# A vision tower on one core: an expert's bias fold summed on VectorE over eight row blocks, then one TensorE product

## The chip, the cores and the metric

The kernel runs on one core of a Trainium2 chip. The metric is device time in microseconds, the median of several executions. The profile comes from one further execution. Its engines are named PE (TensorE), PEld (TensorE's weight loads), DVE (VectorE), ACT (ScalarE), POOL (GpSimd) and SP (SyncE).

## The reference

The input is 64 images; each gives 196 tokens of 256 numbers, 12,544 tokens in all. What is computed, cut to what matters:

```
h  = patches(x) @ W_tok.T + b_tok                      # 768 -> 256
h1 = h + ssm(layernorm(h))                             # Bu, a scan over tokens, y = xs@C + u@D
x2 = layernorm(h1)
y1 = ln1(x2 + mha(x2))                                 # attention over the 64 images, 4 heads
t  = y1[tokens of expert e]                            # top 1 of 8 experts, capacity 1568
hid = t @ w1[e] + b1[e]                                # 256 -> 1024, no activation follows
y  = hid @ w2[e] + b2[e]                               # 1024 -> 256
out = h1 + ln2(y1 + gate * y)
```

Since nothing stands between the two products of an expert, the kernel folds them beforehand: `W12[e] = w1[e] @ w2[e]` (256 x 256), and `b12[e] = b1[e] @ w2[e] + b2[e]` (256). The change is about the second.

## The kernel before

The program has three stages, with a barrier between them: tokens, scan and layer norms (the first, up to about 560 us of the profile), attention and routing, then the experts. Each stage is one block in which every engine runs its own stream of instructions, and semaphores join them. The order on an engine is the order in which its `step` function lists the parts.

The first stage goes over 49 groups of 256 tokens (`NG`), one group per round. An engine's `step(k)` treats several groups at different ages: TensorE in round k turns u of group k-2 into ps_t (L650), makes the outputs ps_y of group k-4, the tokens ps_h of group k in two halves, then a part of a fold (`fold`), then the inputs of the scan ps_b of group k-2. The products of the groups are sums of three fp32r products each (high and low parts), by `product` (L297). In the same round VectorE makes, in this order: nrm_x (L595, L599), the scans xs (L531), the residual h1o from ps_y (L578), nrm_a (L564, L568), ul (L523), h of the first half (L549) and its statistics, sl (L539), the statistics of h1o and mv_xa (L591), h of the second half, its statistics and aggregates (L559). ScalarE makes nrm_x (L438) behind mv_xa, bu from ps_b (L414), xh (L402), sh, uh, x2o and u. GpSimd makes xl in three instructions of 128x512 (L476), hb (L484) and h1b (L492). TensorE needs ul before ps_b, sl before ps_y of the next round, and u before the next ps_t.

The fold runs beside this, six rounds per expert (`FOLD = 6`), for 48 rounds. `k.slot(FOLD)` is the place in the six, called slot here, and `k.turn(FOLD)` the expert. The weights of an expert lie in w1s (w1 transposed) and w2s, 128 partitions x 8 blocks of 256, with b1 behind it as eight columns. Slots 0 and 1 make the first half of W12 in ps_f (four products each, L690), slots 2 and 3 the second. Slots 4 and 5 make the bias: eight products (four each, L694) with the weights b1p (128x2, one column of b1 doubled) and one block of w2s as moving operand, summed into ps_fb (2x256). These products are plain fp32, and each shows in the profile as two records. b1p is copied from w2s by GpSimd in slot 2 (`pair_b1`, L501). The result is added into b12 by VectorE at the end of slot 0 of the next expert (`fold_bias`, L607).

SyncE loads the next expert (`next_expert`): w1s in slot 4 after the last ps_f product; the first half of w2s in slot 5, after slot 4's bias products (`fb_first`); the second half in slot 0, after slot 5's (`fb_ps`). Each of these stands in SyncE's order ahead of the round's xf load and of the two stores of h1b and x2o.

Of the kernel before, what the change touches and what calls it, by code (L numbers as in the profile page):

```python
# [13 lines left out]
P = 128  # L14
# [86 lines left out]
def build(nc, xt, w_tok, b_tok, log_a, w_b, b_b, w_c, b_c, w_d, b_d, log_dt, w_in, b_qk, b_v, w_o, b_o,  # L101
# [4 lines left out]
    with ExitStack() as ctx:  # L106
# [22 lines left out]
        c_eps = sb("c_eps", [P, 1])  # L129
        before = sb("before", [P, P], BF16)  # L130
# [24 lines left out]
        with ExitStack() as pre:  # L155
# [73 lines left out]
            def _(dve):  # L229
# [9 lines left out]
                v.memset(c_eps[:], EPS)  # L239
                v.memset(ones_b[:], 1.0)  # L240
# [63 lines left out]
        with ExitStack() as pa:  # L304
# [26 lines left out]
            b1p = sb("b1p", [P, FK, 2], F32, pa)  # L331
# [14 lines left out]
            b1_pair, w2_first, fb_first = (sem(n) for n in ("fold_b1_pair", "w2_first_loaded", "fold_bias_half"))  # L346
# [5 lines left out]
            def _(sp):  # L352
# [18 lines left out]
                def next_expert(k):  # L371

                    if k.slot(FOLD) == 4:
                        wait(sp, fold_ps, k.turn(FOLD) + 1)
                        sp.dma_start(w1s[:], w1t[k.turn(FOLD) + 1]).then_inc(w1_loaded, 16)
                    elif k.slot(FOLD) == 5:
                        wait(sp, fb_first, k.turn(FOLD) + 1)
                        sp.dma_start(w2s[:, 0:HALF], w2[k.turn(FOLD) + 1, :, 0:HALF]).then_inc(w2_first, 16)
                    elif k.slot(FOLD) == 0:
                        wait(sp, fb_ps, k.turn(FOLD))  # L380
                        sp.dma_start(w2s[:, HALF:], w2[k.turn(FOLD), :, HALF:]).then_inc(w2_loaded, 16)
# [84 lines left out]
            def _(pool):  # L466
# [28 lines left out]
                def pair_b1(k):  # L495
                    if k.slot(FOLD) == 2 and k.valid(FOLD * NE):
                        e = k.turn(FOLD)
                        wait(pool, w2_loaded, (e + 1) * 16)
                        wait(pool, fb_ps, e)
                        apart(pool, passed["pool"])  # L500
                        nc.gpsimd.tensor_copy(b1p[:], w2s[:, FK * D:FK * D + FK].unsqueeze(2)  # L501
                                              .to_broadcast([P, FK, 2])).then_inc(b1_pair, 1)

                def step(k):
                    pair_b1(k)
# [10 lines left out]
            def _(dve):  # L516
# [84 lines left out]

                def fold_bias(k):
                    if k.slot(FOLD) == 0 and k.back(1).valid(FOLD * NE):
# [14 lines left out]
                def step(k):  # L618

                    for m, stage in ((k.back(5), scale_x), (k.back(5), shift_x), (k.back(3), of(scan, 0)),  # L620
# [3 lines left out]
                                     (k, of(hidden, 1)), (k, of(stats_h, 1)), (k, of(mean_h, 0)), (k, of(mean_h, 1)),  # L624
                                     (k, fold_bias)):
                        if m.valid(NG):
                            stage(m)

# [3 lines left out]
            def _(pe):  # L632
# [42 lines left out]
                def fold(k):  # L675
# [22 lines left out]
                    if k.slot(FOLD) == 4:  # L698
                        last.then_inc(fb_first, 1)
                    if k.slot(FOLD) == 5:  # L700
                        last.then_inc(fb_ps, 1)

                def step(k):
# [4 lines left out]
                    if k.valid(NG):  # L708
                        tokens(k, 0)
                        tokens(k, 1)  # L710
                    if k.valid(FOLD * NE):
                        fold(k)
# [817 lines left out]
```

## Time and profile before

| | us |
|---|---|
| median of 3 runs | 1353.25 (1352.43 to 1354.72) |
| the profiled execution | 1356.27 |
| its span, first to last instruction | 1354.4 |
| TensorE busy | 1261.2 (93%) |
| VectorE busy | 1020.7 (75%) |
| ScalarE busy | 737.2 (54%) |
| GpSimd busy | 718.3 (53%) |

Busy times of one engine add up only where its instructions do not overlap; those of different engines run side by side. TensorE's instructions are pipelined: one lasts longer than the distance from its start to the next start, so rounds and folds are measured from start to start. The rounds of the steady part are read in the timeline, each from its ps_t on.

### The profile page before, as it was taken

The numbers are of one execution on the slowest core, as the hardware profiler recorded it, in microseconds if no ns is written. First come the engines' busy times: TensorE is split into PE (matmuls) and PEld (weight loads), VectorE is DVE, ScalarE is ACT, GpSimd is POOL, SyncE is SP. The second block draws the span as 40 slices with busy tenths as digits, with TensorE's granted clock in tenths as the row PEclk, the third lists the DMA queues.
The fourth block names the chain that finished last, engine by engine and source line by source line (L and its number), as shares of the span: only waits on it lengthen the run. The fifth ranks groups of instructions, "written<-read, shape, count | busy, mean of one in ns | idle before, by whom it ended". The sixth has DMA issues, their size and how long they took to land. (4 is left out here: it accounts for less than half of the span.)

```text
span 1354.4 us, 37450 instructions
## 1 busy us (share of the span) xinstructions
PE 1261.2 (93%) x11810; PEld 1147.7 (85%) x11811; DVE 1020.7 (75%) x2787; ACT 737.2 (54%) x1515; POOL 718.3 (53%) x966
## 2 busy tenths in 40 slices
PE   2999999999999999589999999999999984999995
PEld 1999999999999999489999999999999983666663
DVE  4577778887777787747777777777777765699997
ACT  3455555555555555445555555555555541477775
POOL 1655666666656665303444444444444443277776
PEclk9999999999999999889999999999999985999998
DMA  7435454545454543202223322332223224677773
GB/s 235 147 121 168 149 163 132 163 137 178 145 182 117 178 117 98 96 28 83 96 93 101 101 93 96 99 99 95 93 97 101 97 79 133 183 215 234 226 230 121
DMA packets 97044, 180.07 MB, mean 133 GB/s; under 512 B 12319, under 2 KB 62497, under 8 KB 95970
## 3 DMA queue, kind: packets, MB, share of 16 engines
q1 hardware_dynamic: 82244, 138.66, 34.1%
q0 software_dynamic: 13312, 39.75, 8.0%
q10 hardware_dynamic: 1440, 1.07, 0.3%
q8 instruction: 23, 0.38, 0.1%
q14 instruction: 25, 0.20, 0.1%
HBM read 112.69 MB, written 67.80 MB: 133 GB/s over the span
## 5 line engine op out<-in xcount | busy, mean ns | idle before, releaser
L476 POOL TENSOR_TENSOR xl<-xf,xh 128x512 fp32r<-128x512 f32 x141 | 179.2, 1299 | 204.6 <-ACT xh L402 204.6
L297 PE MATMUL ps_h<-wh,xh 128*128 128x256 f32 x588 | 166.3, 283 | 4.9 <-DVE xl L611 4.9
L297 PE MATMUL ps_h<-wh,xl 128*128 128x256 f32 x588 | 166.2, 283 | 0.0
L297 PE MATMUL ps_h<-wl,xh 128*128 128x256 f32 x588 | 166.0, 282 | 0.0
L851 ACT ACTIVATE zn<-z,nm_z,rs_z 128x256 f32<-128x256 f32 x98 | 53.6, 594 | 200.7 <-DVE nm_z L982 200.7
L1323 POOL DMA_INDIRECT out<-res,c_idx x106 | 116.5, 1099 | 61.6 <-issue 46.2
L920 POOL DMA_INDIRECT bins<-rows,slot_i x98 | 100.7, 1028 | 60.1 <-POOL slot_i L914 45.2
L1471 PE MATMUL c_ps_y<-w,yt 128*128 x424 | 116.9, 398 | 6.5 <-issue 4.1
L297 PEld LDWEIGHTS ps_h<-wh,xh 128*128 128x128 f32 x588 | 111.8, 190 | 5.7 <-DVE xl L611 5.7
L297 PE MATMUL b<-x2h,wh 128*128 128x256 f32 x392 | 114.7, 293 | 0.0
L297 PEld LDWEIGHTS ps_h<-wl,xh 128*128 128x128 f32 x588 | 111.7, 190 | 0.0
L297 PEld LDWEIGHTS ps_h<-wh,xl 128*128 128x128 f32 x588 | 111.5, 190 | 0.0
L297 PE MATMUL b<-x2h,wl 128*128 128x256 f32 x392 | 110.8, 283 | 0.0
L297 PE MATMUL b<-x2l,wh 128*128 128x256 f32 x392 | 110.7, 282 | 0.0
L936 DVE TENSOR_TENSOR x2l<-ps_o,x2h 128x512 fp32r<-128x512 f32 x49 | 33.9, 692 | 96.5 <-ACT x2h L856 96.5
L894 POOL TENSOR_TENSOR x2b<-x,rows_c 128x512 f32<-128x512 f32 x49 | 63.4, 1295 | 62.3 <-DVE z L968 58.5
L914 POOL CAST slot_i<-small 128x2 int32<-128x2 f32 x49 | 9.1, 186 | 159.3 <-DVE small L1030 159.3
L1471 PEld LDWEIGHTS c_ps_y<-w,yt 128*128 128x128 f32 x424 | 71.9, 189 | 24.4 <-issue 12.0
L438 ACT ACTIVATE nrm_x<-mv_xa,c_eps 128x2 f32<-128x2 f32 x49 | 14.5, 296 | 141.3 <-DVE mv_xa L591 141.3
L531 DVE TENSOR_TENSOR_SCAN xs<-decay,xs,bu 128x256 f32<-128x256 f32 x96 | 66.9, 738 | 29.8 <-ACT bu L414 29.5
L492 POOL TENSOR_TENSOR h1b<-h1o,rows_c 128x512 f32<-128x512 f32 x49 | 79.4, 1622 | 10.1 <-DVE h1o L578 10.1
L539 DVE TENSOR_TENSOR sl<-xs,sh 128x512 fp32r<-128x512 f32 x49 | 79.8, 1629 | 0.1
(255 smaller groups left out, 4409.4 us busy)
## 6 DMA issues: line engine op xcount, KB each, us to landing
xf<-xt SPq DMA_DIRECT2D x49, 768.0 KB, 5.3
row<-bins SPq DMA_DIRECT2D x106, 257.5 KB
h_dram<-h1b SPq DMA_DIRECT2D x49, 256.0 KB, 5.3
x_dram<-x2o SPq DMA_DIRECT2D x49, 256.0 KB, 5.4
x<-x_dram SPq DMA_DIRECT2D x98, 128.0 KB, 2.8
rows<-h_dram SPq DMA_DIRECT2D x98, 128.0 KB, 2.8
w1s<-w1t SPq DMA_DIRECT2D x8, 1024.0 KB, 6.8
w2s<-w SPq DMA_DIRECT2D x8, 516.0 KB, 5.4
```

The lines of the kernel that those rows point to most:

```text
L297: last = nc.tensor.matmul(out_ps, a, b, start=(i == 0), stop=(i == len(terms) - 1))
L438: nc.scalar.activation(nrm_x[:, 0, :], mv_x[:, :, 1], ACT.Sqrt, bias=c_eps[:]).then_inc(x_sd, 1)
L476: last = nc.gpsimd.tensor_tensor(xl[:, p, part], xf[:, p, part], xh[:, p, part].bitcast(F32), ALU.subtract)
L492: nc.gpsimd.tensor_tensor(h1b[:, p], h1o[:, p], r_be2.unsqueeze(1).to_broadcast([P, 2, D]), ALU.add).then_inc(h1b_done, 1)
L531: v.tensor_tensor_scan(xs[:, p, t, :], decay[:, t, bass.ds(m.n() * G % N, G)], bu[:, p, t, :], 0.0 if first else xs[:, 1 - p, t, G - 1:G], ...
L539: v.tensor_tensor(sl[:, p, :], xs[:, p].rearrange("p t g -> p (t g)"), sh[:, p, :].bitcast(F32), ALU.subtract).then_inc(s_lo, 1)
L851: A(zn[:, s, :], z[:, s, :], ACT.Identity, bias=nm_z[:, s:s + 1], scale=rs_z[:, s:s + 1]).then_inc(Q["zn"], 1)
L894: g.tensor_tensor(x2b[:, p], x2[:, p], r_bo.unsqueeze(1).to_broadcast([P, 2, D]), ALU.add).then_inc(Q["x2b"], 1)
L920: g.indirect_dma_start(bins, bass.IndirectOffsetOnAxis(ap=slot_i[:, p, s:s + 1], axis=0), rows[:, p, s, :], None).then_inc(scattered[p], 16)
L936: v.tensor_tensor(xl[:], b_2, xh[:].bitcast(F32), ALU.subtract).then_inc(Q["x2lo"], 1)
L1323: g.indirect_dma_start(out, bass.IndirectOffsetOnAxis(ap=idx[:, b, i:i + 1], axis=0), res[:, b, i, :], None, bounds_check=S - 1, oob_is_er ...
L1471: mm(ps_y[p][:, i, :], yt[:, p, i, t * P:(t + 1) * P], w12[:, bass.ds(e, 1), t * D:(t + 1) * D].rearrange("p a d -> p (a d)"), start=(t == ...
```

## The change

The sum over the eight row blocks moves off TensorE. VectorE keeps an array acc (128x256). In slots 2 to 5 it does two of eight steps each, `acc = w2s[block f] * b1[f] + acc`, with b1's column as a scalar per partition; the first is a plain product. This part, `sum_bias`, stands first in VectorE's round. TensorE then needs a single product, weights `ones_2` (128x2, all ones) and acc as moving operand, which sums over the partitions (`fold_sum`). It stands in slot 0 of the next expert, ahead of `fold`. `fold_bias` goes from the end of slot 0 to the end of slot 1. GpSimd's `pair_b1` goes. SyncE's two w2s loads wait for the counts of `acc_done` in place of the bias products. The diff, cut to its core:

```diff
+                def sum_bias(k):
+                    if k.slot(FOLD) >= 2 and k.valid(FOLD * NE):
+                        e = k.turn(FOLD)
+                        if k.slot(FOLD) == 2:
+                            wait(dve, w2_first, (e + 1) * 16)
+                            wait(dve, w2_loaded, (e + 1) * 16)
+                            wait(dve, fb_ps, e)
+                        for f in range((k.slot(FOLD) - 2) * 2, (k.slot(FOLD) - 1) * 2):
+                            w, b = w2s[:, f * D:(f + 1) * D], w2s[:, FK * D + f:FK * D + f + 1]
+                            if f == 0:
+                                v.tensor_scalar(acc[:], w, b, None, ALU.mult).then_inc(acc_done, 1)
+                            else:
+                                wait(dve, acc_done, e * FK + f)
+                                v.scalar_tensor_tensor(acc[:], w, b, acc[:], ALU.mult, ALU.add).then_inc(acc_done, 1)
...
                 def fold_bias(k):
-                    if k.slot(FOLD) == 0 and k.back(1).valid(FOLD * NE):
+                    if k.slot(FOLD) == 1 and k.back(2).valid(FOLD * NE):
                         e = k.turn(FOLD) - 1
                         wait(dve, fb_ps, e + 1)
...
-                    if k.slot(FOLD) == 4:
-                        wait(pe, fb_out, e)
-                        wait(pe, b1_pair, e + 1)
-                    for f in range(again * FK // 2, (again + 1) * FK // 2):
-                        if part < FT:
+                    if part < FT:
+                        for f in range(again * FK // 2, (again + 1) * FK // 2):
                             last = nc.tensor.matmul(ps_f[:, part * D:(part + 1) * D],
                                                     w1s[:, f * D + part * P:f * D + (part + 1) * P],
                                                     w2s[:, f * D:(f + 1) * D], start=(f == 0), stop=(f == FK - 1))
-                        else:
-                            last = nc.tensor.matmul(ps_fb[:], b1p[:, f, :], w2s[:, f * D:(f + 1) * D],
-                                                    start=(f == 0), stop=(f == FK - 1))
...
+                def fold_sum(k):
+                    if k.slot(FOLD) == 0 and k.back(1).valid(FOLD * NE):
+                        e = k.turn(FOLD) - 1
+                        wait(pe, acc_done, (e + 1) * FK)
+                        wait(pe, fb_out, e)
+                        nc.tensor.matmul(ps_fb[:], ones_2[:], acc[:], start=True, stop=True).then_inc(fb_ps, 1)
...
                     elif k.slot(FOLD) == 5:
-                        wait(sp, fb_first, k.turn(FOLD) + 1)
+                        wait(sp, acc_done, k.turn(FOLD) * FK + FK // 2)
...
                     elif k.slot(FOLD) == 0:
-                        wait(sp, fb_ps, k.turn(FOLD))
+                        wait(sp, acc_done, k.turn(FOLD) * FK)
```

The lines shift: L297 is L299 in the changed kernel, L690 is L695, L549 is L541, L595 is L587.

TensorE, slot 4, between the last tokens and the inputs of the scan; before:

```order
L297 MATMUL ps_h<-wl,xh 128x256
L297 MATMUL ps_h<-wh,xl 128x256
L694 MATMUL ps_fb<-w2s,b1p 2x256 x4
L297 MATMUL ps_b<-uh,wh 128x256
L297 MATMUL ps_b<-ul,wh 128x256
```

The same place now:

```order
L299 MATMUL ps_h<-wh,xh 128x256
L299 MATMUL ps_h<-wl,xh 128x256
L299 MATMUL ps_h<-wh,xl 128x256
L299 MATMUL ps_b<-uh,wh 128x256
L299 MATMUL ps_b<-ul,wh 128x256
```

Here, and in slot 5 alike, the four products into ps_fb are gone and ps_b follows on ps_h. TensorE, slot 0, the same place; before:

```order
L297 MATMUL ps_h<-wl,xh 128x256
L297 MATMUL ps_h<-wh,xl 128x256
L81 ISA
L81 REGISTER_ALU
L690 MATMUL ps_f<-w2s,w1s 128x256 x4
L81 REGISTER_ALU
L297 MATMUL ps_b<-uh,wh 128x256
L297 MATMUL ps_b<-ul,wh 128x256
```

Now:

```order
L299 MATMUL ps_h<-wl,xh 128x256
L299 MATMUL ps_h<-wh,xl 128x256
L81 ISA
L707 MATMUL ps_fb<-acc,ones 2x256
L81 ISA
L695 MATMUL ps_f<-w2s,w1s 128x256 x4
L81 REGISTER_ALU
L299 MATMUL ps_b<-uh,wh 128x256
L299 MATMUL ps_b<-ul,wh 128x256
```

One product into ps_fb and a wait stand ahead of the four into ps_f. VectorE, from the second h of slot 1 to the start of slot 2's round; before:

```order
L549 TENSOR_TENSOR h<-ps_h,rows_c 128x256
L553 BN_STATS stats_a<-h 128x6
L559 BN_AGGR mv_a<-stats_a 128x2 x2
L595 RECIPROCAL nrm_x<-nrm_x 128x2
L599 SCALAR_TENSOR_TENSOR nrm_x<-mv_xa,nrm_x 128x2
```

Now, with the bias row's add and the first two sums ahead of nrm_x:

```order
L541 TENSOR_TENSOR h<-ps_h,rows_c 128x256
L545 BN_STATS stats_a<-h 128x6
L551 BN_AGGR mv_a<-stats_a 128x2 x2
L81 REGISTER_ALU
L615 ISA
L615 TENSOR_TENSOR b<-ps_fb,b 2x256
L81 ISA
L605 TENSOR_SCALAR acc<-w2s 128x256
L81 ISA
L608 SCALAR_TENSOR_TENSOR acc<-w2s,acc 128x256
L587 RECIPROCAL nrm_x<-nrm_x 128x2
L591 SCALAR_TENSOR_TENSOR nrm_x<-mv_xa,nrm_x 128x2
```

In slots 3, 4 and 5 two sums stand at this place, each behind the one ahead of it; here slot 4's:

```order
L545 BN_STATS stats_a<-h 128x6
L551 BN_AGGR mv_a<-stats_a 128x2 x2
L81 REGISTER_ALU
L608 SCALAR_TENSOR_TENSOR acc<-w2s,acc 128x256
L81 REGISTER_ALU
L608 SCALAR_TENSOR_TENSOR acc<-w2s,acc 128x256
L587 RECIPROCAL nrm_x<-nrm_x 128x2
L591 SCALAR_TENSOR_TENSOR nrm_x<-mv_xa,nrm_x 128x2
```

nrm_x, and the scans behind it, stand two instructions of 128x256 later in these rounds.

## Rows read from the trace of the kernel before

**Rows 1.** Busy us per engine in a stretch; its first line names the columns.

```profile
core 0: us, PE busy (x) PEld busy (x) DVE busy (x) ACT busy (x) POOL busy (x), PEclk, DMA share, GB/s
...
100.00:528.00 428.00, 428.00 (x3343) 404.86 (x3342) 340.05 (x763) 245.51 (x447) 267.23 (x206) 1.00 0.49 151
```

**Rows 2.** Waits, 100 to 500 us: who for whom, total, times, longest.

```profile
DVE h1o L578 <- PE ps_y L297: 39.8, 37, 1.3
```

**Rows 3.** PE timeline, first stage: start, us, engine, line, operation; xcount merged.

```profile
198.40 0.60 PE L650 MATMUL ps_t<-ident,u 128*128 128x128 f32 x4
...
209.36 0.60 PE L650 MATMUL ps_t<-ident,u 128*128 128x128 f32 x4
...
220.04 0.60 PE L650 MATMUL ps_t<-ident,u 128*128 128x128 f32 x4
...
259.51 0.28 PE L297 MATMUL ps_h<-wh,xl 128*128 128x256 f32 x1
259.72 1.89 PE L694 MATMUL ps_fb<-w2s,b1p 128*2 128x256 f32 x8
261.54 0.39 PE L297 MATMUL ps_b<-uh,wh 128*128 128x256 f32 x1
...
263.06 0.60 PE L650 MATMUL ps_t<-ident,u 128*128 128x128 f32 x4
...
532.66 0.60 PE L650 MATMUL ps_t<-ident,u 128*128 128x128 f32 x4
...
541.62 0.60 PE L650 MATMUL ps_t<-ident,u 128*128 128x128 f32 x4
```

**Rows 4.** PE groups by form: count, busy us, mean ns of one.

```profile
L694 PE MATMUL ps_fb<-w2s,b1p 128*2 128x256 f32 x128 | 30.2, 379 | 0.0
```

**Rows 5.** DVE groups by form, the nearest operations.

```profile
L1369 DVE SCALAR_TENSOR_TENSOR cinc<-ps_l,oht 128x392 f32<-128x392 f32 x2 | 1.1, 566 | 0.1
...
L285 DVE TENSOR_TENSOR rows_c<-rows_c 128x256 f32<-128x256 f32 x1 | 0.4, 426 | 0.1
```

**Rows 6.** DVE timeline of the round at 198.40; in brackets idle before, releaser.

```profile
198.37 0.16 DVE L599 SCALAR_TENSOR_TENSOR nrm_x<-mv_xa,nrm_x 128x2 f32<-128x2 f32 x1
199.44 1.39 DVE L531 TENSOR_TENSOR_SCAN xs<-decay,xs,bu 128x256 f32<-128x256 f32 x2 [0.91 <-ACT bu L414]
201.88 0.69 DVE L578 TENSOR_TENSOR h1o<-ps_y,hb 128x512 f32<-128x512 f32 x1 [1.04 <-PE ps_y L297]
...
202.67 1.23 DVE L568 SCALAR_TENSOR_TENSOR nrm_a<-mv_a,nrm_a 128x2 f32<-128x2 f32 x1
203.83 0.68 DVE L523 TENSOR_TENSOR ul<-ps_t,uh 128x512 fp32r<-128x512 f32 x1
...
205.22 1.72 DVE L539 TENSOR_TENSOR sl<-xs,sh 128x512 fp32r<-128x512 f32 x1
...
207.78 0.25 DVE L591 BATCH_NORM_AGGREGATE mv_xa<-stats_x 128x2 f32<-128x6 f32 x2 [0.19 <-DVE stats_x L584]
...
208.74 0.45 DVE L559 BATCH_NORM_AGGREGATE mv_a<-stats_a 128x2 f32<-128x6 f32 x2
```

**Rows 7.** ACT timeline of the same round.

```profile
197.17 0.30 ACT L438 ACTIVATE nrm_x<-mv_xa,c_eps 128x2 f32<-128x2 f32 x1 [3.03 <-DVE mv_xa L591]
198.59 1.02 ACT L414 ACTIVATE bu<-ps_b,cols_c 128x256 f32<-128x256 f32 x2 [1.13 <-PE ps_b L297]
...
199.69 1.48 ACT L402 ACTIVATE xh<-xf 128x1536 fp32r<-128x1536 f32 x1
```

**Rows 8.** POOL timeline of the same round.

```profile
201.34 3.81 POOL L476 TENSOR_TENSOR xl<-xf,xh 128x512 fp32r<-128x512 f32 x3 [4.18 <-ACT xh L402]
205.11 1.28 POOL L484 TENSOR_TENSOR hb<-h,rows_c 128x512 f32<-128x512 f32 x1
206.35 1.72 POOL L492 TENSOR_TENSOR h1b<-h1o,rows_c 128x512 f32<-128x512 f32 x1
```

**Rows 9.** Issues of DMAs by the SP queue, timeline of the same round.

```profile
208.11 0.37 SPq L381 DMA_DIRECT2D w2s<-w  x1
```

More of the change, by code:

```diff
@@ L129, in build @@
         c_eps = sb("c_eps", [P, 1])
+        ones_2 = sb("ones_2", [P, 2])
         before = sb("before", [P, P], BF16)
@@ L239, in _ @@
                 v.memset(c_eps[:], EPS)
+                v.memset(ones_2[:], 1.0)
                 v.memset(ones_b[:], 1.0)
@@ L330, in build @@
             ps_fb = pb("ps_fb", [2, D])
-            b1p = sb("b1p", [P, FK, 2], F32, pa)
+            acc = sb("acc", [P, D], F32, pa)
             h1_stored = [sem(f"h1_stored{i}") for i in range(2)]
@@ L345, in build @@
             h1b_done = sem("a_h1b_done")
-            b1_pair, w2_first, fb_first = (sem(n) for n in ("fold_b1_pair", "w2_first_loaded", "fold_bias_half"))
+            w2_first, acc_done = (sem(n) for n in ("w2_first_loaded", "fold_bias_sum"))
             HALF = FK // 2 * D
@@ L493, in add_out @@
                                             ALU.add).then_inc(h1b_done, 1)
[L495 to L502, printed above, removed]
                 def step(k):
-                    pair_b1(k)
                     if k.back(5).valid(NG):
@@ L618, in step @@
                 def step(k):
-                    for m, stage in ((k.back(5), scale_x), (k.back(5), shift_x), (k.back(3), of(scan, 0)),
+                    for m, stage in ((k, sum_bias), (k.back(5), scale_x), (k.back(5), shift_x), (k.back(3), of(scan, 0)),
                                      (k.back(3), of(scan, 1)), (k.back(4), residual), (k.back(1), scale_h),
@@ L623, in step @@
                                      (k.back(3), split_s), (k.back(4), stats_x), (k.back(4), mean_x),
-                                     (k, of(hidden, 1)), (k, of(stats_h, 1)), (k, of(mean_h, 0)), (k, of(mean_h, 1)),
-                                     (k, fold_bias)):
+                                     (k, of(hidden, 1)), (k, of(stats_h, 1)), (k, of(mean_h, 0)), (k, of(mean_h, 1))):
                         if m.valid(NG):
                             stage(m)
+                    fold_bias(k)
                 run(dve, step, 0, NG + 5, 6, 42, FOLD)
@@ L692, in fold @@
                                                     w2s[:, f * D:(f + 1) * D], start=(f == 0), stop=(f == FK - 1))
-                        else:
-                            last = nc.tensor.matmul(ps_fb[:], b1p[:, f, :], w2s[:, f * D:(f + 1) * D],
-                                                    start=(f == 0), stop=(f == FK - 1))
                     if k.slot(FOLD) == 3:
                         last.then_inc(fold_ps, 1)
[L698 to L701, printed above, removed]
+                def fold_sum(k):
[4 more added lines that the diff above has]
+                        nc.tensor.matmul(ps_fb[:], ones_2[:], acc[:], start=True, stop=True).then_inc(fb_ps, 1)
                 def step(k):
@@ L710, in step @@
                         tokens(k, 1)
+                    fold_sum(k)
                     if k.valid(FOLD * NE):
```

## The prediction

> **What bounds the kernel now.** I read first the busy times by stretch [rows 1]. Between 100 and 528 us, the steady part of the first stage, TensorE is busy for 428.00 of 428.00 us at a granted clock of 1.00, VectorE for 340.05. In the list of waits for 100 to 500 us TensorE has no row as an engine that waits; VectorE waits for it, 37 times in 39.8 us [rows 2]. So this stage is as long as TensorE's instructions, and what goes from TensorE goes from the time, until another engine's round becomes longer. The second thing to read is how far that is.
>
> One round of the stage (one group of 256 tokens) starts with the turn of u (ps_t). I call that instant T and take all places in a round from it. Turns start at 198.40, 209.36 and 220.04 us [rows 3]: the round at 198.40 is a slot 5 (four products into ps_fb) and takes 10.96 us; the one at 209.36 is a slot 0 (four products into ps_f) and takes 10.68. The last round with tokens, 532.66 to 541.62, has no fold and takes **8.96 us** [rows 3]. So a fold into ps_f costs 1.72 us and one into ps_fb costs 2.00 us. Eight records of ps_fb span 1.89 us [rows 3] and one lasts 0.379 [rows 4], so they follow each other at (1.89 - 0.38)/7 = 0.216, and eight are 1.73: a fold into ps_f costs just that. With ps_fb come 0.27 us of switches, of which 0.09 on the way in (259.51 to 259.72, where 0.12 is the usual step) and the rest on the way out to ps_b. The two-column weights make the switches dearer.
>
> **TensorE.** There are 128 records of ps_fb [rows 4], two per product: 8 products x 8 experts. The change takes them from slots 4 and 5: 2 x 2.00 = 4.00 us per expert. It adds in slot 0 one product, two records: 2 x 0.216 = 0.43, with all the switches 0.70. I take 0.60, nearer the upper end, because the switch out goes to weights of 128 columns as before, though to ps_f's and not to ps_b's. Net 4.00 - 0.60 = 3.40 us per expert, **27.2 us for eight**. Its bounds are 26.4 and 28.6.
>
> **VectorE's price.** No row has a multiply-add over 128x256 in SBUF. The nearest: 128x256 with both operands in SBUF took 426 ns, a scalar_tensor_tensor over 128x392 took 566 ns [rows 5]. The eight form a chain through acc; the dearest such link in the trace is 0.19 us idle (mv_xa behind stats_x [rows 6]). I take 0.44 us each, near the first row because it has the same shape, **0.88 us per round in slots 2 to 5**; the bounds are 0.35 (half of h1o's 0.69 for 128x512 [rows 6]) and 0.57 plus a link, 0.76. In all 64 x 0.44 = 28 us of added work on VectorE.
>
> **Slots 2 and 3.** VectorE's round: residual h1o at T+3.5 (it waited 1.04 us for ps_y), mv_xa at T+9.4, the last aggregates end at T+10.8, then nrm_x and the scans, which waited 0.91 us for bu [rows 6]. Without waiting, residual to nrm_x is 7.25 us and nrm_x and the scans to the next residual 1.63, so VectorE's own round is 8.88. With the sum 9.76, under 10.68: the scans slip about 0.2 us, the residual none. Cost nothing. (In slot 2 the add into the bias row, two partitions of 256 and no dearer than a sum, now ends the round before: 10.2, still under.)
>
> **Slots 4 and 5, where the cover is thin.** TensorE's round is now 8.96 and VectorE's with a sum 9.76. I walk from T4 (start of slot 4), with T5 = T4+8.96 and T0 = T5+8.96. Slot 4's residual is still on time; its VectorE round ends at T4+10.8 = T5+1.84. The sum runs to T5+2.72, nrm_x to 3.03, scans to 4.40, residual at 4.41 instead of about 3.5: **0.9 us late**. ScalarE is late too: its nrm_x waits for mv_xa (T4+9.7 = T5+0.7), so bu, and xh behind it [rows 7], start 0.8 late, and GpSimd's xl at T5+3.8 instead of 2.95 [rows 8].
> What catches this up is a wait that the trace already has. nrm_a, 128x2, took 1.23 us though a nrm_x of the same shape took 0.16: it was asked at 202.67, just after GpSimd's first xl ended (201.34 + 1.27), and ended at 203.90 with the second [rows 6, 8]. sl likewise ends 0.55 us after hb ends [rows 6, 8]. Both end at the limits of GpSimd's instructions, whenever they were asked. In slot 5 these limits lie at T5+3.8 plus multiples of 1.27, so nrm_a ends at 6.3 (asked at 5.2, after the limit at 5.07), ul at 6.95 and sl at 3.8+5.04+0.55 = 9.39. The twelve products into ps_b fill the last 1.52 us of a round (261.54 to 263.06 [rows 3]), so TensorE wants ul at T5+7.4 (slack 0.5); it wants sl at T0+0.36 = T5+9.32: **a stall of about 0.1 us**, some 0.15 with the semaphore. In slot 0 TensorE's round is 10.68+0.6 = 11.3 and VectorE has no sum, so all is on time again by T1. Stalls: 8 x 0.15 = 1.2 us.
>
> **The rest.** GpSimd loses eight copies of 128x16; nobody waits for what stands behind them, GpSimd itself waits over 4 us for xh in a round [rows 8]. SyncE's two w2s loads now wait for sums of VectorE that end before the products they waited for: the second was issued at 208.11 [rows 9], would go out some 1 us earlier, and is needed by TensorE a round and a half later. Behind them in SyncE's queue stand xf loads and stores, which come no later. The last bias row moves one round into the drain, where TensorE already waits: up to 0.4 us lost with VectorE's last lag.
>
> **The sum** against the profiled execution's span, 1354.4: 27.2 - 1.2 - 0.4 = 25.6, so 1328.8. Later stages do not see the change. The run of that profile took 1356.27, 3.0 above the median 1353.25; I take the same difference off the median: **1327.6 us**.
>
> **A rule against the change.** The trace shows VectorE's two-operand SBUF instructions stopped by GpSimd's [rows 6, 8], by up to 1.07 us. The Trainium skill, page "SBUF — State Buffer", section "SBUF: two separate sides", says the same: the shared port pair goes as an exclusive lock to whichever starts first, for its whole instruction, when VectorE has two SBUF inputs. All seven later sums per expert have two. By the lock each could cost a GpSimd instruction more; by the places worked out above none does.
>
> **Rivals.**
> (a) *The sums meet the lock: slower.* If every sum waited 1.07 us, the pair would cost about 0.88 + 2.14 = 3.0 us and VectorE's round 8.88+3.0 = 11.9. Slots 2 and 3 would take 1.2 us more each than now, 4 and 5 0.9 each, slot 0 0.6, less about 1.2 that the slack before sl takes up: +3.6 per expert, +29 us, 1382. For it: the rule, and that GpSimd is busy 6.7 of 10.96 us of a round. Against: GpSimd's round ends at 208.07 and its next xl starts 2.95 us after T, while the sums lie at T+0.1 to T+1.0, in slot 5 at T+1.84 to T+2.72. It decides from where the sums start some 1.1 us later than I have them in slot 5, 2 us in slots 2 to 4.
> (b) *The two short rounds become VectorE's.* If the sums cost 0.76 each, or nrm_a or sl miss one GpSimd limit more (1.27 us), slots 4 and 5 run at 9.8 to 10.1 us, and TensorE loses 1 to 1.7 us per expert more: 8 to 14 us given back, 1335 to 1341. For it: 9.76 is over 8.96, and two short rounds follow each other. Against: as the round is now, ul ends at T+6.1 and sl at T+8.5, so in a round without fold 1.3 and 0.8 us are left before TensorE wants them, and a dearer sum is still taken up by the same GpSimd limits.
> (c) *Nothing moves*, because another engine holds the rounds at 10.7. Against: every engine but TensorE has waits in each round. 1351 to 1355.
>
> **Chances.** Forecast with its bounds (1324 to 1331; 28.6 us with no stall gives 1324.6) 0.70; between it and (b) 0.06; (b) 0.14; (a) 0.03; (c) 0.02; cheaper than all bounds 0.05. The range 1324 to 1337 takes in the forecast and the nearer part of (b) and leaves out 0.18. A measurement of this kernel tells about 0.2% from no change: faster by more 0.95, within 0.02, slower 0.03.
>
> **What would show it.** Per expert, four rounds of 10.7 us, two near 9.0 and slot 0 near 11.3. 16 records of ps_fb instead of 128. The sums at 0.42 to 0.45 us each, with no 1.2 us ones among them: those would be (a). TensorE waiting for sl at the start of slot 0, 0.1 to 0.2 us; waits of 1 us there, or for ul, would be (b). nrm_a in slot 5 shorter than elsewhere. I am wrong if the stage ends less than 20 us earlier.

## The result, and the profile after

The changed kernel took a median of **1320.45 us** (1319.77 to 1321.81), the kernel before 1352.95 on the same chip: a ratio of 0.9759 [0.9742 to 0.9776]. 32.5 us went, where 25.6 were forecast; 1320.45 lies under the range's lower end of 1324.0. The profiled execution has a span of 1318.9 us and took 1320.70.

Busy us by engine from 100 to 500 us, after (columns as in [rows 1]), and from the list of waits for the same stretch (as [rows 2]):

```profile
100.00:500.00 400.00, 400.00 (x3235) 391.18 (x3234) 332.13 (x807) 240.47 (x440) 270.29 (x198) 1.00 0.51 160
```

```profile
DVE h1o L570 <- PE ps_y L299: 20.1, 29, 1.3
```

TensorE still fills the stage at a granted clock of 1.00 and waits for nobody in this list; VectorE's wait for it has halved, from 39.8 to 20.1 us. The bound is the same as before.

PE timeline of one expert after, the counterpart of [rows 3]: turns of u in slots 1, 2, 4, 5, 0 and 1, with the fold of slot 1 and, in slot 0, the single product at its head.

```profile
209.56 0.60 PE L658 MATMUL ps_t<-ident,u 128*128 128x128 f32 x4
...
217.07 1.89 PE L695 MATMUL ps_f<-w2s,w1s 128*128 128x256 f32 x8
218.61 0.47 PE L299 MATMUL ps_b<-uh,wh 128*128 128x256 f32 x1
...
220.22 0.60 PE L658 MATMUL ps_t<-ident,u 128*128 128x128 f32 x4
...
241.51 0.60 PE L658 MATMUL ps_t<-ident,u 128*128 128x128 f32 x4
...
250.44 0.60 PE L658 MATMUL ps_t<-ident,u 128*128 128x128 f32 x4
...
259.06 0.60 PE L658 MATMUL ps_t<-ident,u 128*128 128x128 f32 x4
...
266.21 0.28 PE L299 MATMUL ps_h<-wh,xl 128*128 128x256 f32 x1
266.42 0.59 PE L707 MATMUL ps_fb<-acc,ones 128*2 128x256 f32 x2
266.94 1.99 PE L695 MATMUL ps_f<-w2s,w1s 128*128 128x256 f32 x8
268.58 0.47 PE L299 MATMUL ps_b<-uh,wh 128*128 128x256 f32 x1
...
270.19 0.60 PE L658 MATMUL ps_t<-ident,u 128*128 128x128 f32 x4
```

A round with a ps_f fold takes 10.65 us, slot 4 8.93, slot 5 8.62 and slot 0 11.13. One expert takes 270.19 - 209.56 = 60.63, against 64.66 before (198.40 to 263.06 [rows 3]): 4.03 us less, where the sum had 3.40 - 0.15 = 3.25. The 8.62 was in no term of the prediction: a round without a fold took 8.96 before [rows 3].

Groups by form of the changed parts (count, busy us, mean ns):

```profile
L707 PE MATMUL ps_fb<-acc,ones 128*2 128x256 f32 x16 | 4.7, 378 | 0.0
...
L608 DVE SCALAR_TENSOR_TENSOR acc<-w2s,acc 128x256 f32<-128x256 f32 x56 | 28.2, 504 | 1.1
L605 DVE TENSOR_SCALAR acc<-w2s 128x256 f32<-128x256 f32 x8 | 3.5, 436 | 0.0
```

16 records of ps_fb stand where 128 did [rows 4]. The sums took 31.7 us of VectorE in all: 0.50 each, not 0.44, but for the first of an expert, the plain product, which took 0.44.

Slot 5 on VectorE after, from 250.44 on (counterpart of [rows 6]):

```profile
251.08 1.02 DVE L608 SCALAR_TENSOR_TENSOR acc<-w2s,acc 128x256 f32<-128x256 f32 x2
...
253.86 0.66 DVE L570 TENSOR_TENSOR h1o<-ps_y,hb 128x512 f32<-128x512 f32 x1
...
256.65 1.44 DVE L531 TENSOR_TENSOR sl<-xs,sh 128x512 fp32r<-128x512 f32 x1
```

The residual starts at T5+3.42, not at the 4.41 I had walked to, and sl ends 0.97 us before the next turn at 259.06 (256.65 + 1.44). TensorE waits for neither in this expert.

To compare stages I take the time from the third turn of the stage (58.10 us before, 59.10 after) to the last turn behind tokens (541.62 before [rows 3], 511.62 after): **483.52 us before, 452.52 after**. 31.0 of the 32.5 us lie there.

### The profile page after: what moved, and what is told of

It is laid out like the page before. It is cut to its first block and busy times, and to the rows that moved or that the text cites. A ratio compares the mean times of both kernels' runs of the same rounds, so it can differ in the third digit from the quotient of the medians.

```text
span 1318.9 us, 37326 instructions
## 1 busy us (share of the span) xinstructions
PE 1225.3 (93%) x11698; PEld 1132.0 (86%) x11699; DVE 1016.6 (77%) x2852; ACT 735.8 (56%) x1515; POOL 738.2 (56%) x958
## 5 line engine op out<-in xcount | busy, mean ns | idle before, releaser
L478 POOL TENSOR_TENSOR xl<-xf,xh 128x512 fp32r<-128x512 f32 x141 | 184.4, 1337 | 171.6 <-ACT xh L404 171.6
L299 PE MATMUL ps_h<-wh,xh 128*128 128x256 f32 x588 | 165.9, 282 | 5.0 <-DVE xl L619 5.0
L299 PE MATMUL ps_h<-wl,xh 128*128 128x256 f32 x588 | 165.3, 281 | 0.0
L299 PE MATMUL ps_h<-wh,xl 128*128 128x256 f32 x588 | 165.3, 281 | 0.0
L1330 POOL DMA_INDIRECT out<-res,c_idx x106 | 123.3, 1163 | 43.3 <-issue 21.4
L1478 PE MATMUL c_ps_y<-w,yt 128*128 x424 | 117.8, 400 | 2.5 <-ACT yt L1277 1.0
L299 PEld LDWEIGHTS ps_h<-wh,xh 128*128 128x128 f32 x588 | 112.3, 191 | 5.7 <-DVE xl L619 5.7
L299 PE MATMUL b<-x2h,wh 128*128 128x256 f32 x392 | 114.7, 293 | 0.0
L299 PEld LDWEIGHTS ps_h<-wl,xh 128*128 128x128 f32 x588 | 112.2, 191 | 0.0
L299 PEld LDWEIGHTS ps_h<-wh,xl 128*128 128x128 f32 x588 | 111.5, 190 | 0.0
L299 PE MATMUL b<-x2l,wh 128*128 128x256 f32 x392 | 110.9, 283 | 0.0
L299 PE MATMUL b<-x2h,wl 128*128 128x256 f32 x392 | 110.8, 283 | 0.0
L486 POOL TENSOR_TENSOR hb<-h,rows_c 128x512 f32<-128x512 f32 x49 | 75.0, 1530 | 9.7 <-DVE h1o L570 9.7
L416 ACT ACTIVATE bu<-ps_b,cols_c 128x256 f32<-128x256 f32 x98 | 49.9, 559 | 51.6 <-PE ps_b L299 51.6
L494 POOL TENSOR_TENSOR h1b<-h1o,rows_c 128x512 f32<-128x512 f32 x49 | 71.2, 1454 | 9.9 <-DVE h1o L570 9.9
```

Source lines behind the costliest of these rows:

```text
L299: last = nc.tensor.matmul(out_ps, a, b, start=(i == 0), stop=(i == len(terms) - 1))
L416: nc.scalar.activation(bu[:, m.slot(2), t, :], ps_b[:, t * G:(t + 1) * G], ACT.Identity, bias=c_bbdt[:, t:t + 1], scale=c_dt).then_inc(bu_ ...
L478: last = nc.gpsimd.tensor_tensor(xl[:, p, part], xf[:, p, part], xh[:, p, part].bitcast(F32), ALU.subtract)
L486: nc.gpsimd.tensor_tensor(hb[:, m.slot(3)], h[:, p], r_bcd.unsqueeze(1).to_broadcast([P, 2, D]), ALU.add).then_inc(hb_done, 1)
L494: nc.gpsimd.tensor_tensor(h1b[:, p], h1o[:, p], r_be2.unsqueeze(1).to_broadcast([P, 2, D]), ALU.add).then_inc(h1b_done, 1)
L1330: g.indirect_dma_start(out, bass.IndirectOffsetOnAxis(ap=idx[:, b, i:i + 1], axis=0), res[:, b, i, :], None, bounds_check=S - 1, oob_is_er ...
```

## Experiments

Times are medians, with the kernel before timed beside them: 1352.23, 1352.63 and 1352.54 us in the three groups of runs. "Stage" is the stretch just defined.

| kernel | us | ratio to before | stage |
|---|---|---|---|
| before / profiled again | 1352.4 | 0.9998 [0.9987, 1.0009] | 483.52 / 483.52 |
| e1_place | 1348.59 | 0.9969 [0.9957, 0.9980] | 479.87 |
| e3_idle_sums | 1348.43 | 0.9968 [0.9956, 0.9980] | 479.94 |
| after | 1320.45 | 0.9759 [0.9742, 0.9776] | 452.52 |
| e2_no_sums | 1321.33 | 0.9759 [0.9737, 0.9782] | 452.41 |
| e9_no_bias | 1319.69 | 0.9760 [0.9744, 0.9776] | 449.89 |
| e8_fold_last | 1321.57 | 0.9769 [0.9748, 0.9789] | 451.50 |
| e4_two_folds | 1323.76 | 0.9781 [0.9761, 0.9801] | 455.93 |
| e5_sums_midround | 1366.53 | 1.0100 [1.0078, 1.0123] | 495.12 |
| e10_plus128 | 1324.30 | 0.9786 [0.9770, 0.9803] | 455.51 |
| e6_unaligned | 1324.67 | 0.9786 [0.9766, 0.9806] | 459.01 |
| e7_aligned | 1328.15 | 0.9812 [0.9793, 0.9832] | 462.65 |
| e11_plus64 | 1328.19 | 0.9824 [0.9808, 0.9841] | 462.53 |

### The kernel before with the new array alone

```diff
         c_eps = sb("c_eps", [P, 1])
+        ones_2 = sb("ones_2", [P, 2])
...
                 v.memset(c_eps[:], EPS)
+                v.memset(ones_2[:], 1.0)
```

> The kernel before with one edit: the 128x2 array ones_2 is declared and set to 1 once, and nothing uses it, so that every array behind it in SBUF lies 8 bytes further on, as in the changed kernel. Theory 'place': the step from one fp32r product to the next (118.6 ns in a round of before, 117.9 in most rounds of after) and the 5 us by which the two later stages were shorter in the profile of after come from where the arrays lie. Then here the step is 117.9, a round with ps_f lasts 10.65 instead of 10.68, and the time is 1348 to 1351. Rival 'no place': 1352 to 1354, step 118.6, rounds 10.68.

Measured: 1348.59 us, 3.6 less than before, with not one instruction of the stage changed. Its turns of u at slot 4, slot 5 and slot 0, and the first and the last of the 36 products into ps_h in that slot 5:

```profile
187.53 0.60 PE L652 MATMUL ps_t<-ident,u 128*128 128x128 f32 x4
...
198.41 0.60 PE L652 MATMUL ps_t<-ident,u 128*128 128x128 f32 x4
...
201.59 0.28 PE L299 MATMUL ps_h<-wh,xh 128*128 128x256 f32 x1
...
205.55 0.28 PE L299 MATMUL ps_h<-wh,xl 128*128 128x256 f32 x1
...
209.10 0.60 PE L652 MATMUL ps_t<-ident,u 128*128 128x128 f32 x4
```

Slot 5 takes 10.69 us, 10.97 before. Products into ps_h follow each other at (205.55 - 201.59)/35 = 0.1131 us here. The same two products in before (slot 4), in after's slot 1, and in after's slot 5:

```profile
255.36 0.28 PE L297 MATMUL ps_h<-wh,xh 128*128 128x256 f32 x1
...
259.51 0.28 PE L297 MATMUL ps_h<-wh,xl 128*128 128x256 f32 x1
```

```profile
212.83 0.28 PE L299 MATMUL ps_h<-wh,xh 128*128 128x256 f32 x1
...
216.95 0.28 PE L299 MATMUL ps_h<-wh,xl 128*128 128x256 f32 x1
...
253.61 0.28 PE L299 MATMUL ps_h<-wh,xh 128*128 128x256 f32 x1
...
257.58 0.28 PE L299 MATMUL ps_h<-wh,xl 128*128 128x256 f32 x1
```

4.15, 4.12 and 3.97 us for 35 steps: 118.6, 117.7 and 113.4 ns. The rows are rounded to 0.01 us; the unrounded starts give 118.5, 117.8 and 113.3 (in e1 113.3 too), and these are used from here on. In before all rounds of the stage have 118.5; in e1 eight of them have 113.3 and the others 117.8. All at a granted clock of 1.00. So moving the arrays changed how fast TensorE's products follow each other, and 3.6 of the 32.5 us have nothing to do with the fold.

### The sums, taken out and put in

e2_no_sums is the changed kernel without `sum_bias` and without SyncE's and TensorE's waits for its counts; the product adds up an acc of zeros, so the bias fold is missing from its result. e3_idle_sums is e1_place with `sum_bias` at its place and TensorE waiting for its counts, but the bias still folded by the eight products.

```diff
-                    for m, stage in ((k, sum_bias), (k.back(5), scale_x), ...
+                    for m, stage in ((k.back(5), scale_x), ...
```

> The changed kernel without VectorE's eight sums per expert: acc is set to zero once, the single product into ps_fb stays (the part b1 @ w2 of the bias is left out). Theory 'rounds without a fold': TensorE's step of 113.3 ns in slots 5 and 0 of after comes from TensorE's own stream having no plain fp32 fold in the round before; it stays here, and the time is 1319 to 1321, since the sums were covered but for some 0.6 us in the last expert. Rival 'VectorE': the short step comes with VectorE's sums or its later places in those rounds; then the step is 117.9 in all rounds here and the time is 1323 to 1326.

> The kernel before with VectorE's eight sums per expert added (and ones_2, acc), their result unused; TensorE keeps its eight bias products and waits for the sums' counts in slots 4 and 5. Theory: the sums are covered by VectorE's waits, rounds stay at 10.65 to 10.97 us and the time equals that of the kernel before with ones_2 alone, within 1 us. Rival 'lock': if sums meet GpSimd's instructions, rounds of slots 2 to 5 grow and the time is over 1356. Rival 'VectorE': if the sums bring TensorE's short step, it shows here too (113.3 ns in some rounds) and the time is under 1347.

Measured: 1321.33, against 1320.45 with the sums, and 1348.43, against 1348.59 without. Both agree within their intervals and their stages within 0.11 us. In long rounds (e3) 31.7 us of added VectorE work cost nothing. In short ones (e2) the agreement is in part chance: in the last expert's slot 5 and the slot 0 behind it the changed kernel takes 9.05 and 9.63 us where e2 takes 8.62 and 9.41, 0.65 more, and it gets 0.53 back by two rounds with the short step that e2 does not have (8.63 and 10.40 in the first expert's slot 5 and the next slot 1, 8.92 and 10.64 in e2). In the six experts between, the sums cost nothing. Rival (b) has no room left with the arrays where they are here; other places follow below.

### The sums where GpSimd works

e5_sums_midround moves `sum_bias` from the head of VectorE's round to just ahead of `split_s` (sl).

```diff
-                    for m, stage in ((k, sum_bias), (k.back(5), scale_x), ...
+                    for m, stage in ((k.back(5), scale_x), ...
...
-                                     (k.back(3), split_s), ...
+                                     (k, sum_bias), (k.back(3), split_s), ...
```

> The changed kernel with the two sums of a round moved to the middle of VectorE's round, ahead of sl, where GpSimd works on xl and hb. Theory 'lock': each sum waits for the end of a GpSimd instruction, a pair costs 2 to 2.6 us instead of 0.95, VectorE's round in slots 2 to 5 becomes about 11, and the time is 1332 to 1348. Rival: place does not matter, sums take 0.48 us each and the time is 1320 to 1322.

Measured: 1366.53 us, 46 more than the changed kernel and 14 more than before, and above the 1332 to 1348 that was expected of the lock. Its groups of sums, TensorE's longest wait from 100 to 500 us, a slot 3's sums on VectorE with GpSimd beside them, and the turns of its slots 5, 0 and 1:

```profile
L608 DVE SCALAR_TENSOR_TENSOR acc<-w2s,acc 128x256 f32<-128x256 f32 x56 | 77.2, 1378 | 1.1
L605 DVE TENSOR_SCALAR acc<-w2s 128x256 f32<-128x256 f32 x8 | 9.8, 1219 | 0.0
```

```profile
PE ps_y L299 <- DVE sl L531: 24.6, 12, 2.5
```

```profile
252.76 2.82 DVE L608 SCALAR_TENSOR_TENSOR acc<-w2s,acc 128x256 f32<-128x256 f32 x2
```

```profile
253.84 1.45 POOL L486 TENSOR_TENSOR hb<-h,rows_c 128x512 f32<-128x512 f32 x1
```

```profile
265.94 0.60 PE L658 MATMUL ps_t<-ident,u 128*128 128x128 f32 x4
...
276.93 0.60 PE L658 MATMUL ps_t<-ident,u 128*128 128x128 f32 x4
...
292.56 0.60 PE L658 MATMUL ps_t<-ident,u 128*128 128x128 f32 x4
```

A sum with two operands in SBUF takes 1.38 us in place of 0.50 while GpSimd runs. Slot 4 and slots 1 to 3 still keep their time (8.93 and 10.65), but slot 5 grows to 10.99 and slot 0 to 15.63 (in the expert before, 12.60 and 12.46), and TensorE waits up to 2.5 us for sl. What takes the time past the expectation is in the clock's record, here behind the wait that ended at 280.03 (columns as in [rows 1]):

```profile
281.40:284.80 3.40, 3.40 (x19) 3.40 (x18) 2.58 (x8) 2.71 (x5) 0.79 (x1) 0.50 0.68 255
```

The granted clock is 0.50 for some 3.4 us, the lower of its two levels (1.2 and 2.4 GHz), and the products follow each other at 213 ns. That happens five times in this stage, at or just behind the end of five of TensorE's twelve waits of over 2 us, and never in the stage of the changed kernel. Some 16 products each time at 0.1 us more are an estimate of 8 of the 46 us. This is rival (a)'s mechanism and sign, at a place where the sums were put to meet it. Its size was 29 us over before, 14 measured: it had all rounds but slot 1 lose, and here only slots 5 and 0 do. It is the rule quoted in the prediction from the Trainium skill, page "SBUF — State Buffer", section "SBUF: two separate sides": the lock is held for a whole instruction. This trace agrees: the pair above took 2.82 us and ended at 255.58, 0.3 us behind GpSimd's hb (253.84 + 1.45), where pairs at the head of the round took 1.02. The first step, which has one array operand and a column of scalars, is stopped just the same (1.22 against 0.44).

### The fold at other places

e8_fold_last puts `fold_sum` and `fold` behind the scan's inputs; e4_two_folds puts the sixteen ps_f products of an expert in two rounds of eight (slots 1 and 2), with four sums in each of them.

```diff
-                    fold_sum(k)
-                    if k.valid(FOLD * NE):
-                        fold(k)
                     if k.back(2).valid(NG):
                         inputs(k.back(2))
+                    fold_sum(k)
+                    if k.valid(FOLD * NE):
+                        fold(k)
```

```diff
-                    e, part = k.turn(FOLD), k.slot(FOLD) // 2
-                    again = k.slot(FOLD) % 2
+                    e, part = k.turn(FOLD), k.slot(FOLD) - 1
...
-                    if part < FT:
-                        for f in range(again * FK // 2, (again + 1) * FK // 2):
+                    if 0 <= part < FT:
+                        for f in range(FK):
...
-                        for f in range((k.slot(FOLD) - 2) * 2, (k.slot(FOLD) - 1) * 2):
+                        for f in range((k.slot(FOLD) - 1) * 4, k.slot(FOLD) * 4):
```

> The changed kernel with the fold and the single product behind ps_b, next to the fp32 transposes ps_t of the next round, in place of ahead of ps_b. If the 0.27 us of switches around products with two-column weights, or the 0.2 us pause between the first two ps_b after a fold, go with the neighbour, eight slots 0 save up to 0.3 us each and the 32 ps_f rounds up to 0.1: 1315 to 1319; VectorE gets bu 1.7 us earlier and nobody waits. If the price lies in the fold itself: 1320 to 1321. If ul comes too late for ps_b (ul ends at T+6.2, ps_b starts at T+7.55): not over 1322.

> The changed kernel with the fold in two rounds of eight products (slots 1 and 2) in place of four of four, and VectorE's sums in the same two rounds, four each. If TensorE's step of 113 ns comes in rounds that follow a round without a fold, slots 4, 5 and 0 have it instead of 5 and 0, one more round of 0.3 us per expert: 1317 to 1319. If VectorE's own round of 8.9 us then sets four rounds in a row of 8.6 to 8.9: 1320 to 1326. If the short step has to do with the slot and the place of the arrays (e1 had it in slot 5 behind a round with ps_fb products), the time is 1319 to 1322 and the step can be read round by round.

Measured: 1321.57 us for e8, the same as after within the intervals; no gain came, and of the cases expected the last fits (ul too late, not over 1322). The short step is in other rounds now: slots 1 and 3 take 10.34 us at 113.3 ns, and slot 5 is back at 117.8 ns with 8.92 us, or 9.29 in four experts where TensorE waits. e4 took 1323.76, 3.3 more than after, where 1317 to 1319 was the first theory. Rounds with eight ps_f products take 12.37, but in four experts slot 2 takes 12.93 to 12.96, since VectorE, with four sums ahead of its round, makes ul too late: 2.3 of the 3.4 us by which the stage is longer. The 8.63 us rounds come irregularly, in 6 of its 24 rounds of slots 3 to 5. Neither beats the changed kernel.

### What the product costs

e9_no_bias is the changed kernel without sums, product and the add of the bias row, and without SyncE's waits for the sums, so that the bias fold is missing from its result.

```diff
-                    for m, stage in ((k, sum_bias), (k.back(5), scale_x), ...
+                    for m, stage in ((k.back(5), scale_x), ...
...
-                    fold_bias(k)
...
-                    fold_sum(k)
```

> The changed kernel without any of the bias fold's first part: no sums, no single product, no add into b12 (b1 @ w2 is left out of the output). It prices what the change added: rounds of slot 0 lasted 11.13 us in after with TensorE's short step and 11.38 without, against 10.65 of the other ps_f rounds, so the product costs 0.73. Theory: the product is the only thing added that is not covered: 8 x 0.73 = 5.8 us less than after, 1313.5 to 1316, slot 0 at 10.35 to 10.65. If the sums cost too (lags, stalls): 1310 to 1313.

Measured: 1319.69 us, 0.8 less than after and not the 4.5 to 7 that was expected, though the product costs 11.38 - 10.65 = 0.73 us in each of eight slots 0 (rounds of equal step, e2_no_sums too). The rest came back another way: all rounds of e9 are 8.92 or 10.65 us, at 117.8 ns; not one short step. After has seven rounds with a short step that gives 0.30 us and seven with 0.25, 3.8 us in all, and TensorE's waits of 0.65 in its last expert: 8 x 0.73 - 3.8 + 0.65 = 2.7, where the stages differ by 2.63 (452.52 - 449.89).

### Other places for the arrays

Four kernels are the changed one with unused arrays of 32 bytes in front of xh and what stands behind it (e7: one also in front of `ident`).

```diff
+        pad_1 = sb("pad_1", [P, 2])
         before = sb("before", [P, P], BF16)
```

> The changed kernel with one more unused array ahead of the others, so that xh and all behind it lie 32 bytes further on. Theory 'place': what e1 gained goes here: the step is 118.6 ns, a round with ps_f 10.68 us, slot 5 about 8.96, the time 1323.5 to 1326. Rival (the gain belongs to one layout of the kernel before alone): 1319 to 1322.

> The changed kernel with two unused arrays, so that ident and decay start at a multiple of 64 bytes too, and xh and all behind it at a multiple of 256. Theory 'place, every array': the transposes with ident, and the products, get a little shorter or stay: 1315 to 1320. If only the multiple of 64 of xh and its kin matters: 1320 to 1321.5.

> The changed kernel with xh and all behind it 128 bytes further on. The rule to test: what counts is the start of xh and its kin modulo 128: 64 in after (1320.5), 96 in e6 (1324.7), 0 in e7 (1328.2). Then this is after again: rounds of 10.65 and 8.62, 1319.5 to 1321.5. If another part of the address counts, the time is anything from 1316 to 1329 and its rounds differ from after's.

> The changed kernel with xh and all behind it 64 bytes further on (a multiple of 256), ident and decay where they were. It parts what e7 moved: if e7's 1328.2 comes from xh and its kin, this is 1327 to 1329; if it comes from ident or decay, this is 1319 to 1322.

Measured, by where xh starts (its byte in the partition, modulo 256):

| kernel | xh at, mod 256 | us | step of ps_h, ns | slots 4, 5, 0, other |
|---|---|---|---|---|
| before | 160 | 1352.4 | 118.5 | 10.97, 10.97, 10.68, 10.68 |
| e1_place | 192 | 1348.59 | 117.8, 113.3 | 10.89 to 10.94, 10.69, 10.65, 10.65 |
| after | 192 | 1320.45 | 117.8, 113.3 | 8.93, 8.62, 11.13, 10.65 |
| e10_plus128 | 64 | 1324.30 | 117.8 | 8.89, 8.89, 11.37, 10.61 to 10.65 |
| e6_unaligned | 224 | 1324.67 | 117.3, 118.7 | 8.92 to 8.99, 8.92 to 9.31, 11.36 to 11.72, 10.64 to 10.72 |
| e7_aligned | 0 | 1328.15 | 118.7, 120.0 | 8.98, 9.27 to 9.30, 11.69 to 11.71, 10.71 to 10.80 |
| e11_plus64 | 0 | 1328.19 | 118.7, 120.0 | 8.98 to 9.00, 9.27 to 9.30, 11.70 to 11.76, 10.70 to 10.74 |

The last column is read from the third expert to the seventh, 180 to 490 us.

One computation in five arrangements, 7.7 us from the best to the worst; their stages differ by up to 10.1. The expectation for e7 missed (no slower than after), and e6 has the expected time, but with 118.7 ns in part of its rounds only. e11 shows that e7's loss comes with xh and what follows it, not with `ident`. e10 was to show whether the start modulo 128 decides; it keeps the 117.8 but has no short step, so that rule falls.

Not all of the loss is the step. In e7 and e11 slot 5 takes 0.30 us longer than slot 4, with the same products in it. Slot 5 of e11_plus64, from its turn to the next one and TensorE's first product behind the transposes, the nrm_a of the slot 4 ahead of it, its scans, and GpSimd's xl:

```profile
191.88 0.60 PE L660 MATMUL ps_t<-ident,u 128*128 128x128 f32 x4
...
201.16 0.66 PE L660 MATMUL ps_t<-ident,u 128*128 128x128 f32 x4
201.78 0.38 PE L301 MATMUL ps_y<-wh,uh 128*128 128x256 f32 x1
```

```profile
187.18 1.29 DVE L562 SCALAR_TENSOR_TENSOR nrm_a<-mv_a,nrm_a 128x2 f32<-128x2 f32 x1
...
195.13 2.38 DVE L525 TENSOR_TENSOR_SCAN xs<-decay,xs,bu 128x256 f32<-128x256 f32 x2 [0.18 <-issue]
```

```profile
195.62 4.24 POOL L480 TENSOR_TENSOR xl<-xf,xh 128x512 fp32r<-128x512 f32 x3 [2.98 <-ACT xh L406]
```

The scans took 1.39 us in before and 2.38 here, where GpSimd's xl starts within them. VectorE is late for the rest of the round, ScalarE's u with it: the turn at 201.16 waits 0.30 us for u, and the first ps_y, 0.62 behind the turn where 0.36 is usual, waits 0.26 for sl. So it goes in the second to the seventh expert of e7 and e11, 0.56 us each and 3.7 with the first and the last. This is the stall of the prediction's walk. Whether it comes goes with nrm_a of slot 4: 1.29 to 1.31 us in those experts of e7 and e11, 0.16 in the same ones of after and e10. In e6 both are found in one run: 0.16 in the three of them with a step of 117.3 ns, 1.31 in the three with 118.7. None of these kernels was run without the sums, so that the stall is their price is argued from the walk and not shown.

### The kernel before once more

> The kernel before, profiled once more. The first profile's span was 1354.4, while after's and most of the experiments' last stage is 188.3 us and its own 191.6, and the second stage 576 to 579.5 against 580.7. If those are the scatter of one execution, this profile has a span of 1350 to 1352 with rounds of 10.68 and 10.97 as before. If they belong to the kernel, its last stage is 191 to 192 again.

The kernel before, unchanged, profiled again: 1352.44 us, stage 483.52, the same to the hundredth. Its span is 1350.0, not 1354.4. The later stages differ; ScalarE's x2h of the second stage, before and before again (count, ns, first and last start):

```profile
L856 ACT ACTIVATE x2h<-ps_o x49: 597/607/610, 573.9 to 1089.6; 128x512 fp32r<-128x512 f32 x49
```

```profile
L856 ACT ACTIVATE x2h<-ps_o x49: 596/607/608, 575.2 to 1089.2; 128x512 fp32r<-128x512 f32 x49
```

515.7 and 514.0 us, and 513.3 in after, of one and the same work; what stands behind it adds the rest. Single executions of before ran from 1350.6 to 1356.8 us. The first profile was taken of a long one.

## Why the prediction was right and wrong

**Right: what bounds the stage, and the fold's price.** At nearly equal steps (e1_place against after: 10.89 and 10.94 us with four bias products, 8.92 without a fold) the products cost 1.97 to 2.02 us a slot, forecast 2.00 each, with the switches that [rows 3] showed.

**Right: the sums are hidden, but for the last expert, and why.** e2 and e3 show it, with 0.65 us left there; e5 shows what covers them: the same sums some 6 us later in the round (252.76 in a slot 3 that began at 246.37) cost 46 us. The size was low by an eighth (0.50 for 0.44, pairs 1.02 for 0.88), without an effect that these runs could part from the rest.

**Mis-sized: the product**, 0.73 for 0.60, above my upper bound of 0.70: -1.0 us for eight. At its own place it costs what I took: from the last ps_h record to the first of ps_f 0.73 us (266.21 to 266.94), of which 0.12 is the usual step. But the fold behind it then lasts 0.10 longer, 1.64 us to the first ps_b (266.94 to 268.58) against 1.54 in slot 1 (217.07 to 218.61).

**Failed: the walk through slots 4 and 5**, which had VectorE 0.9 us late and sl stalling TensorE by 0.15 us per expert, 1.2 in all; it was 0.65, all of it in the last expert. I let nrm_a end at GpSimd's limits "whenever they were asked". Slots 2, 3 and 5 after, nrm_a on VectorE and xl on GpSimd:

```profile
224.57 0.16 DVE L560 SCALAR_TENSOR_TENSOR nrm_a<-mv_a,nrm_a 128x2 f32<-128x2 f32 x1
...
235.21 1.25 DVE L560 SCALAR_TENSOR_TENSOR nrm_a<-mv_a,nrm_a 128x2 f32<-128x2 f32 x1
...
254.63 0.42 DVE L560 SCALAR_TENSOR_TENSOR nrm_a<-mv_a,nrm_a 128x2 f32<-128x2 f32 x1
```

```profile
223.25 3.93 POOL L478 TENSOR_TENSOR xl<-xf,xh 128x512 fp32r<-128x512 f32 x3 [3.93 <-ACT xh L404]
...
233.89 3.80 POOL L478 TENSOR_TENSOR xl<-xf,xh 128x512 fp32r<-128x512 f32 x3 [3.79 <-ACT xh L404]
...
253.38 4.17 POOL L478 TENSOR_TENSOR xl<-xf,xh 128x512 fp32r<-128x512 f32 x3 [2.08 <-ACT xh L404]
```

nrm_a takes 0.16, 1.25 and 0.42 us. Where it is short, GpSimd's three xl are 0.13 and 0.37 longer than 3.80: VectorE slipped in between two of them, at the limit that I had it miss (223.25 + 1.27 = 224.52; 253.38 + 1.27 = 254.65). In slot 4, on which slot 5's start hangs, nrm_a took 0.16 in six experts of eight. There the VectorE round ends 1.1 us earlier than I walked it, and slot 5's residual starts at T+3.42 to 3.47. In the first and the last expert it took 1.17, and there VectorE is late as I had it, but not by my amount: residual at T+4.14 and T+5.32, where I had 4.41, and sl 0.27 us before the next turn and 0.51 after it. The last one, slot 5 from its turn at 492.94 to the next at 501.99:

```profile
495.83 2.51 DVE L523 TENSOR_TENSOR_SCAN xs<-decay,xs,bu 128x256 f32<-128x256 f32 x2
498.26 0.66 DVE L570 TENSOR_TENSOR h1o<-ps_y,hb 128x512 f32<-128x512 f32 x1
...
500.93 1.57 DVE L531 TENSOR_TENSOR sl<-xs,sh 128x512 fp32r<-128x512 f32 x1
```

That round took 9.05 us where e2's, at the same step of 113.3 ns, took 8.62. The scans are what the walk left out. It had them run to T5+4.40 and GpSimd's xl start at T5+3.8, and priced no meeting; here they took 2.51 us and not 1.39, with xl starting at 496.50 within them, as in e7 and e11. So the walk's mechanism exists, its stall is 0.56 to 0.65 us and not 0.15 where it comes, and here it came in one expert of eight. By e7 and e11, and by nrm_a's 1.30 us in six slots 4 of before, it may well have come in most experts with the arrays where they were before; no run of the fold there shows it. That it did not is luck as far as the prediction goes.

The drain's 0.4 us was not lost either: TensorE's last ps_y ends 20.57 us behind the last turn with tokens, 20.77 before. Errors of the sum: -1.0 (product) + 0.55 (stalls, 0.65 for 1.2) + 0.4 (drain) leave 25.6 at 25.55. The stages give the same (next paragraph but one), so the sum came out right with three terms that were wrong and cancel.

**Also off, without effect:** the second w2s load. I had it issued 1 us earlier; it went at T+9.55 of slot 5, against T+9.71.

**Missing: the step that put the time outside the range.** The prediction priced the declaration of `ones_2` at nothing, and did so without a word: no term of its sum stands for it, and the rounds without a fold went in at the 8.96 us of before. It is 3.65 us of the stage (e1_place, run with nothing else changed), and another 1.8 because after has more rounds with the short step than e1 (3.8 us of them against 2.0); that second part is read from the rounds, not parted by a run. The stages differ by 31.0, so 25.55 is left for the fold, its product and its stalls: what the forecast had at 25.6. Without these two the time would have been 1325.9 or so, inside the range.

**The base was right.** I carried over the difference of 3.0 between profile and median as it stood. e12 shows it to be one execution's later stages, not the kernel's, so taking it off was right; an argument from the spans alone (1354.4 - 1318.9 = 35.5) would overstate the gain by 3 us.

**Open.** 1.5 of the 32.5 us lie outside the stage measured here; later stages of one kernel differ by as much from one execution to the next. Why TensorE's step takes several values (113.3, 117.3 to 117.8, 118.5 to 120.0) is not settled. That short rounds are those without a fold fell with e9 (none among its rounds) and with e1 (one behind ps_fb's products); that xh's start modulo 128 decides fell with e10. What the rows show is that in after the step settles within the first products of ps_y behind a turn and then holds up to the next turn or fold: slot 0 at 259.06 has 113.3 ns up to its fold and 117.8 behind it. Which of the arrays behind `ones_2` it is that matters was not tried.

## What to carry to other kernels

A new array, however small, moves what stands behind it: run the kernel before with the declaration alone, and price the edit against that one. On a stage that one engine fills to 100%, a per cent of that engine's step is worth as much as an instruction. Added VectorE work with SBUF operands was free here where GpSimd rests and took nearly three times its length where GpSimd works, so the place in the round mattered more than the amount. When a walk through a round ends with a margin of tenths of a microsecond, follow every instruction with operands in SBUF through it, the scans too: one meeting with GpSimd was up to 1.1 us here.

## What the hardware showed

- The start of arrays in SBUF, shifted by 32 to 128 bytes, moved TensorE's step between fp32r products of 128x256 among 113.3, 117.3 to 117.8 and 118.5 to 120.0 ns at the same granted clock. The changed kernel moved with it by up to 7.7 us (1320.45 to 1328.19) and its stage by up to 10.1 (452.52 to 462.65), of which 3.7 are TensorE's waits.
- A VectorE multiply-add over 128x256 in SBUF took 0.50 us with GpSimd idle and 1.38 with GpSimd busy; two scans of 128x256 took 1.39 and, with GpSimd's xl starting within them, 2.38 to 2.51. A 128x2 multiply-add that started within 0.05 us of the end of a GpSimd instruction took 0.16, 0.42 or 1.25 us. Nothing in the trace shows what decides.
- A single plain product with two-column weights between products of 128 columns cost 0.73 us, though its two records span 0.59; 0.10 of it appeared only behind the next eight records.
- In e5_sums_midround TensorE waited over 2 us in a round twelve times, and five times the granted clock then stood at 0.50 for some 3.4 us, with products 213 ns apart. In the changed kernel's stage, without such waits, it stayed at 1.00.
